# First attention of a four-layer stack: row sums from the exponentials' accumulator, rows scaled by GpSimd ahead of their transposes

## What is computed

```python
x = x + tanh(g_xattn[0]) * _L0_xattn_ref(_layernorm(x), ctx_1024, ctx_1024, mask, wq, wk, wv, wo, bo)

def _L0_xattn_ref(q, k, v, mask, wq, wk, wv, wo, bo):
    HEAD = 16                      # 16 heads of 16 columns
    qh = (q @ wq).reshape(N, Lq, HEAD, HEAD_DIM)
    kh = (k @ wk).reshape(N, Lk, HEAD, HEAD_DIM)
    vh = (v @ wv).reshape(N, Lk, HEAD, HEAD_DIM)
    scores = jnp.einsum('nqha,nkha->nhqk', qh, kh)
    scores = jnp.where(mask == 0, -10000000000.0, scores)
    attn = softmax(scores / math.sqrt(HEAD_DIM), axis=-1)
    out = jnp.einsum('nhqk,nkha->nqha', attn, vh).reshape(N, Lq, D_MODEL)
    return out @ wo + bo
```

## Time and profile before

| | |
|---|---|
| Median of three runs | 1626.49 us |
| Span of the profiled execution | 1600.8 us |
| TensorE busy with matmuls, whole span | 1386.6 us (87%) |
| VectorE, ScalarE, GpSimd busy, whole span | 60%, 42%, 26% |
| Layer 0's attention | the first 195 us or so |

### The profile page before, as it was taken

One profiled execution on the slowest core, in us unless ns is written; L12 is line 12 of the kernel. 1 busy time (PEld: TensorE's weight loads), 2 busy tenths in 40 slices (PEclk: granted clock), 3 DMA queues, 4 the chain that ended last, 5 costly groups with the idle time before them and its releaser, 6 DMA issues. The chain is left out here.

```text
span 1600.8 us, 31601 instructions
## 1 busy us (share of the span) xinstructions
PE 1386.6 (87%) x10662; PEld 1150.0 (72%) x10662; DVE 953.2 (60%) x2331; ACT 664.8 (42%) x1313; POOL 422.6 (26%) x578
## 2 busy tenths in 40 slices
PE   8999878889999994999999998999999997401588
PEld 5888645677799983788888887779999996400245
DVE  4888665666422225777777774832222265688887
ACT  3666453420344430333333334335555522430277
POOL 1000000012122210122221221246666633421141
PEclk9999999899799997999999998889999999755799
DMA  3000020673111107111111202012333344421001
GB/s 107 21 20 15 6 92 1 218 268 61 60 34 41 34 22 226 62 51 49 49 47 32 44 1 93 1 52 92 92 93 93 86 173 134 108 19 10 1 14 40
DMA packets 105328, 106.53 MB, mean 67 GB/s; under 512 B 36080, under 2 KB 92160, under 8 KB 105088
## 3 DMA queue, kind: packets, MB, share of 16 engines
q1 hardware_dynamic: 89312, 70.91, 14.6%
q0 software_dynamic: 11136, 28.93, 6.6%
q10 hardware_dynamic: 4768, 5.25, 1.1%
HBM read 83.19 MB, written 20.71 MB: 65 GB/s over the span
## 5 line engine op out<-in xcount | busy, mean ns | idle before, releaser
L3598 PEld LDWEIGHTS L2f_bank<-L2f_xT,L2f_w_tile 128*128 128x128 f32 x1264 | 154.5, 193 | 7.4 <-ACT L2f_xT L3662 3.4
L3598 PE MATMUL L2f_bank<-L2f_xT,L2f_w_tile 128*128 128x128 f32 x1264 | 155.2, 276 | 3.0 <-ACT L2f_xT L3662 3.0
L785 POOL TENSOR_TENSOR L2x_probs<-L2x_probs,L2x_inv_sum 128x512 f32<-128x512 f32 x64 | 66.3, 1057 | 268.4 <-DVE L2x_inv_sum L1062 268.4
L3712 DVE TENSOR_TENSOR L2f_hT<-L2f_gate_h,L2f_bank 128x256 f32<-128x256 f32 x79 | 33.3, 421 | 148.5 <-ACT L2f_gate_h L3669 148.5
L3521 POOL DMA_INDIRECT L2f_y_rows<-L2f_xn,L2f_put_row x79 | 78.2, 989 | 55.2 <-DVE L2f_xn L3728 51.6
L3656 ACT COPY L2f_w_tile<-L2f_w_up 128x1024 f32 x79 | 82.7, 1046 | 17.4 <-issue 17.4
L3513 POOL DMA_INDIRECT L2f_rows<-L2f_x_rows,L2f_take_row x79 | 77.0, 975 | 44.7 <-DVE L2f_take_row L3496 21.3
L3598 PEld LDWEIGHTS L1f_bank<-L1f_xT,L1f_w_tile 128*128 128x128 f32 x736 | 85.6, 192 | 1.1
L3598 PE MATMUL L1f_bank<-L1f_xT,L1f_w_tile 128*128 128x128 f32 x736 | 85.9, 275 | 0.0
L3615 PE MATMUL L1f_bank<-L1f_w_down,L1f_hT 128*128 x368 | 83.1, 379 | 0.0
L3615 PE MATMUL L2f_bank<-L2f_w_down,L2f_hT 128*128 x316 | 81.4, 380 | 0.1
(11 more groups left out here) (677 smaller groups left out, 3321.2 us busy)
## 6 DMA issues: line engine op xcount, KB each, us to landing
L1f_w_up<-in_L_ffn_w SPq DMA_DIRECT2D x16, 512.0 KB, 8.2
L1f_w_down<-in_L_ffn_w SPq DMA_DIRECT2D x16, 512.0 KB, 9.0
L2f_got<-L2f_y_rows SPq DMA_DIRECT2D x16, 512.0 KB, 4.4
L2f_w_up<-in_L_ffn_gate_w SPq DMA_DIRECT2D x16, 256.0 KB, 2.9
L2f_w_up<-in_L_ffn_up_w SPq DMA_DIRECT2D x16, 256.0 KB, 3.0
L2f_w_down<-in_L_ffn_down_w SPq DMA_DIRECT2D x16, 256.0 KB, 3.6
x<-in_x SPq DMA_DIRECT2D x4, 512.0 KB, 7.9
L0x_ctx<-in_ctx SPq DMA_DIRECT2D x16, 128.0 KB, 2.1
```

What stands on the lines that cost most here:

```text
L785: nc.gpsimd.tensor_tensor(probs[c][:, :, :], probs[c][:, :, :], inv_sum[:, c, :][:, :, None].to_broadcast([P, 4, P]), ALU.mult).then_inc(s ...
L3598: x = nc.tensor.matmul(products(j, m), w_tile[j][:, at:at + P], xT[j][:, k * P:(k + 1) * P], start=(k == 0), stop=(k == KT - 1))
L3712: nc.vector.tensor_tensor(hT[j][:, 0:F], gate_h[j][:, 0:F], bank[2 + j][:, F:2 * F], ALU.mult).then_inc(q["h"], 1)
```

## The change

- `exp` is four instructions, one a head, each with an accumulator output that gives the sum of its row (`row_sum`). The exponentials have four buffers instead of two, and wait for GpSimd's reading of the batch before.
- VectorE takes the reciprocals of these sums (`invert`, 128x4), at four places of its list.
- GpSimd multiplies each group by them (`weigh_rows`) into `weights`, and the transposes read these.
- The product with ones, its operand, its memsets, and the 128x256 reciprocal are gone; `take_heads` is a plain copy.
- The lists are reordered: transposes 2 and 3 of a batch stand behind the scores of the next, front(b+2, T) stands ahead of transposed(b, 1), and ScalarE's copies move likewise.

```diff
--- before.py
+++ after.py
@@ -300,7 +300,8 @@
-        ones32 = sb(f"{tag}_ones32", [P, 2, 32])
+        row_sum = sb(f"{tag}_row_sum", [P, 4, 4])
+        inv_sum = sb(f"{tag}_inv_sum", [P, 4, 4])
@@ -311,16 +312,16 @@
-        probs = [sb(f"{tag}_probs{j}", [P, 4, P]) for j in range(2)]
+        probs = [sb(f"{tag}_probs{j}", [P, 4, P]) for j in range(4)]
+        weights = [sb(f"{tag}_weights{j}", [P, 4, P]) for j in range(2)]
-        inv_sum = sb(f"{tag}_inv_sum", [P, D])
-            "inv", "headsT", "projected", "updated", "passed", "gated_bias", "x_biased"])
+            "inv", "weights", "headsT", "projected", "updated", "passed", "gated_bias", "x_biased"])
@@ -359,26 +360,35 @@
             nc.gpsimd.memset(mask_diag[:, :], 0.0).then_inc(s["diag"], 1)
             for j in range(2):
                 nc.gpsimd.memset(v32[j][:, :, :, :], 0.0).then_inc(s["cleared"], 1)
-            nc.gpsimd.memset(ones32[:, :, :], 0.0).then_inc(s["cleared"], 1)
 
             pool.wait_ge(s["diag"], 1)
             nc.gpsimd.affine_select(out=mask_diag[:, :], in_=mask_diag[:, :], compare_op=ALU.not_equal,
                                     fill=L0_MASK["diag"], base=0, pattern=[[-1, P]],
                                     channel_multiplier=1).then_inc(s["diag"], 1)
 
-            pool.wait_ge(s["cleared"], 3)
-            for odd in range(2):
-                nc.gpsimd.memset(ones32[:, odd, odd * HD:(odd + 1) * HD], 1.0).then_inc(s["cleared"], 1)
-
             def add_bias(j, b, first, last):
 
                 pool.wait_ge(s["xn"], b + 1)
                 nc.gpsimd.tensor_tensor(cols(core.x, b * D, D), cols(core.x, b * D, D), gated_bias[:, :], ALU.add
                                         ).then_inc(s["x_biased"], 1)
 
+            def weigh_rows(b, i):
+
+                pool.wait_ge(s["inv"], b * 4 + (i + 1))
+                after(pool, s["pT"], b * 4 + (i - 1))
+                nc.gpsimd.tensor_tensor(weights[i % 2][:, :, :], probs[i][:, :, :],
+                                        inv_sum[:, i, :][:, :, None].to_broadcast([P, 4, P]), ALU.mult
+                                        ).then_inc(s["weights"], 1)
+
+            def body(j, b, first, last):
+                weigh_rows(b, 0)
+                weigh_rows(b, 1)
+                add_bias(j, b, first, last)
+                weigh_rows(b, 2)
+                weigh_rows(b, 3)
 
             pool.wait_ge(s["gated_bias"], 1)
-            over_batches(pool, add_bias)
+            over_batches(pool, body)
 
         @block.tensor
         def _(pe):
@@ -429,10 +439,10 @@
 
             def transposed(b, i):
 
-                pe.wait_ge(s["exped"], b * 4 + (i + 1))
+                pe.wait_ge(s["weights"], b * 4 + (i + 1))
                 after(pe, s["pT_out"], b * 4 + (i - 1))
                 for h in range(4):
-                    last = nc.tensor.transpose(pT_bank[i % 2][:, h * P:(h + 1) * P], probs[i % 2][:, h, :],
+                    last = nc.tensor.transpose(pT_bank[i % 2][:, h * P:(h + 1) * P], weights[i % 2][:, h, :],
                                                core.ident[:, :])
                 last.then_inc(s["pT"], 1)
 
@@ -441,14 +451,12 @@
                 pe.wait_ge(s["pT_out"], b * 4 + 4)
                 pe.wait_ge(s["evicted"], b * NF + (V + 1))
                 after(pe, s["updated"], b)
-                for at, stationary in ((0, lambda t, i, odd: v32[j][:, 4 * t + i, odd, :]),
-                                       (D, lambda t, i, odd: ones32[:, odd, :])):
-                    for t in range(KT):
-                        for odd in range(2):
-                            for i in range(4):
-                                last = nc.tensor.matmul(out_bank[32 * i:32 * i + 32, at + t * P:at + (t + 1) * P],
-                                                        stationary(t, i, odd), probsT[j][:, i, 2 * t + odd, :],
-                                                        start=(odd == 0), stop=(odd == 1))
+                for t in range(KT):
+                    for odd in range(2):
+                        for i in range(4):
+                            last = nc.tensor.matmul(out_bank[32 * i:32 * i + 32, t * P:(t + 1) * P],
+                                                    v32[j][:, 4 * t + i, odd, :], probsT[j][:, i, 2 * t + odd, :],
+                                                    start=(odd == 0), stop=(odd == 1))
                 last.then_inc(s["pv"], 1)
 
             def project(j, b):
@@ -462,6 +470,7 @@
             def body(j, b, first, last):
                 scores(j, b)
                 if not first:
+                    transposed(b - 1, 2)
                     transposed(b - 1, 3)
                 if has_two_before(b):
                     project(j, b - 2)
@@ -474,16 +483,15 @@
                 transposed(b, 0)
                 if not last:
                     front(1 - j, b + 1, V)
-                transposed(b, 1)
-                transposed(b, 2)
                 if not two_left(b):
                     front(j, b + 2, T)
+                transposed(b, 1)
 
 
             pe.wait_ge(prologue.sems["cleared"], 2)
             stay_warm(core, out_bank, 10)
             pe.wait_ge(s["diag"], 2)
-            pe.wait_ge(s["cleared"], 5)
+            pe.wait_ge(s["cleared"], 2)
             front(0, 0, T)
 
             pe.wait_ge(s["w_q"], 16)
@@ -496,6 +504,7 @@
 
             pe.wait_ge(s["w_o"], 32)
             over_batches(pe, body)
+            transposed(B - 1, 2)
             transposed(B - 1, 3)
             project(0, B - 2)
             weighted(1, B - 1)
@@ -530,9 +539,11 @@
             def exp(b, i):
 
                 act.wait_ge(s["shifted"], b * 4 + (i + 1))
-                after(act, s["pT"], b * 4 + (i - 1))
-                nc.scalar.activation(probs[i % 2][:, :, :], shifted[i % 2][:, :, :], ACT.Exp, scale=scale
-                                     ).then_inc(s["exped"], 1)
+                after(act, s["weights"], (b - 1) * 4 + (i + 1))
+                for h in range(4):
+                    e = nc.scalar.activation(probs[i][:, h, :], shifted[i % 2][:, h, :], ACT.Exp, scale=scale,
+                                             accum_out=row_sum[:, i, h:h + 1])
+                e.then_inc(s["exped"], 1)
 
             def take_pT(j, b, i):
 
@@ -543,6 +554,7 @@
 
             def body(j, b, first, last):
                 if not first:
+                    take_pT(1 - j, b - 1, 2)
                     take_pT(1 - j, b - 1, 3)
                 exp(b, 0)
                 if not last:
@@ -552,11 +564,10 @@
                 exp(b, 2)
                 if not last:
                     take(1 - j, b + 1, V)
-                take_pT(j, b, 1)
                 exp(b, 3)
-                take_pT(j, b, 2)
                 if not two_left(b):
                     take(j, b + 2, T)
+                take_pT(j, b, 1)
 
             prologue.on_scalar(act)
             finish_norm_scalar(core, act, s, temps)
@@ -569,6 +580,7 @@
             take(0, 0, V)
             take(1, 1, T)
             over_batches(act, body)
+            take_pT(1, B - 1, 2)
             take_pT(1, B - 1, 3)
             nc.scalar.preload_act_table(ACT.Sqrt)
 
@@ -598,15 +610,17 @@
                                         top[:, i % 2, :][:, :, None].to_broadcast([P, 4, P]), ALU.subtract
                                         ).then_inc(s["shifted"], 1)
 
+            def invert(b, i):
+
+                dve.wait_ge(s["exped"], b * 4 + (i + 1))
+                after(dve, s["weights"], (b - 1) * 4 + (i + 1))
+                nc.vector.reciprocal(inv_sum[:, i, :], row_sum[:, i, :]).then_inc(s["inv"], 1)
+
             def take_heads(j, b):
 
                 dve.wait_ge(s["pv"], b + 1)
-                nc.vector.reciprocal(inv_sum[:, :], out_bank[:, D:2 * D]).then_inc(s["inv"], 1)
-
-                dve.wait_ge(s["inv"], b + 1)
                 after(dve, s["projected"], b - 1)
-                nc.vector.tensor_tensor(headsT[j][:, :], out_bank[:, 0:D], inv_sum[:, :], ALU.mult
-                                        ).then_inc(s["headsT"], 1)
+                nc.vector.tensor_copy(headsT[j][:, :], out_bank[:, 0:D]).then_inc(s["headsT"], 1)
 
             def update(b):
 
@@ -621,11 +635,16 @@
             def body(j, b, first, last):
                 if not two_left(b):
                     norm(j, b + 2)
+                if not first:
+                    invert(b - 1, 2)
+                    invert(b - 1, 3)
                 shift(b, 0)
                 if has_two_before(b):
                     update(b - 2)
                 shift(b, 1)
+                invert(b, 0)
                 shift(b, 2)
+                invert(b, 1)
                 shift(b, 3)
                 if not first:
                     take_heads(1 - j, b - 1)
@@ -648,6 +667,8 @@
             nc.vector.tensor_scalar(gated_bias[:, :], bo[:, :], core.gate(layer, 0), None, ALU.mult
                                     ).then_inc(s["gated_bias"], 1)
```

(2 more changed lines are left out.)

## The result

The changed kernel is slower. Its median over 4 runs is 1656.05 us (1651.04 to 1656.68), against 1626.96 (1623.12 to 1628.2) of the kernel before beside it: a ratio of 1.0157 [1.0126, 1.0188], +29 us. A second comparison on another occasion gave 1656.52 against 1629.62, 1.0188 [1.0152, 1.0224]. The forecast was 1663 us. What came is near the time of rival 1 (1654): the walked beat of 11.85 us came as 11.82, and the loss of clock that was added to it (+9) didn't take place in the steady part.

A forecast was written before the change was run, and what follows sets the result against it. TensorE was taken to bound layer 0's attention. The profiled span 1600.8 + 27.5 (beats +25.5, stage's end about +2) + 9 for the clock = 1637.3, plus 25.7 from span to median = 1663 us; range 1645 to 1683.

The forecast's parts named there:

- rival 1: Layer 0's attention: slower as walked, without any loss of clock, 1654 us; chance 0.20.
- the walked beat: Layer 0's attention, one batch followed through the engines' queues: 11.85 us against 10.14, +1.7 a batch, +25.5 over 15 beats.
- The bound: Layer 0's attention before the change: TensorE is the bound, with a beat of 10.14 us a batch.
- An exp group: ScalarE: four 128x128 exponentials with accumulator reads take 1.23 us against 0.53, +0.70 a group, +2.8 a batch.
- GpSimd's multiplication: GpSimd, between exp and transpose: four broadcast multiplications of 128x512 at 1.06 us each, 4.2 a batch.
- The memsets: Start of the kernel: five small memsets leave while TensorE warms up, worth nothing.
- The clock term: Layer 0's attention, steady part: TensorE's thin stretch loses clock, 0.6 us a beat, +9 us.
- Rival 2: Layer 0's attention: the clock falls in nearly every beat, some +1.5 a beat, +50, 1676 us; chance 0.17.
- The stage's end: End of layer 0's attention: longer groups +2.8, a VectorE and GpSimd round +1.4, less 2.6: about +2 us.
- Rival 3: Layer 0's attention: TensorE stays the bound as ScalarE takes V early enough; beat 9.25, -13, 1613 us; chance 0.09.
- Rival 4: ScalarE alone sets the beat: its work sums to 8.6 us, under TensorE's 9.25; falls together with rival 3.
- Rival 5: Accumulator reads merged or reciprocals stalled: beat 11.2 to 12.3, 1645 to 1661 us; lower end or mixed cases 0.04.

The follow-up runs named there:

- the change without GpSimd: Changed kernel without GpSimd's multiplication, the transposes reading the exponentials and the rows left undivided: 1663.48 us, ratio 1.018 to the kernel before.
- the old order: Changed kernel's operations with TensorE's and ScalarE's queues in the order of the kernel before: 1681.07 us, ratio 1.0315 to the kernel before.
- the reordered kernel: Changed kernel's same operations, with transposes 1 also behind the next scores and the fills and takes moved earlier: 1622.68 us, again 1625.97.
- one exponential: Changed kernel with one 128x512 exponential a group instead of four, no accumulator, sums a constant 1: 1650.01 us, ratio 1.0097 to the kernel before.
- multiplication twice: Changed kernel with each GpSimd multiplication made twice, the first into a tile nobody reads: 1694.26 us, ratio 1.0379 to the kernel before.

## Why the prediction was right, and where it was wrong

**The bound.** That TensorE bounds the kernel before is shown by the kernel without the product with ones: 0.89 us of work removed, 0.85 of beat gained.

**The walk.** Its stations, counted from the scores' start at 105.83, can be read off the timelines above: take of q and k 4.89 (walked 4.84), exp 1 5.87 (5.82), copy of transposes 0 7.62 (7.6), exp 2 8.10 (8.1), take of V 9.28 (9.3), front T 9.93 (9.85), next scores 11.85 (11.7). The mean of 11.85 was the 11.7 and half of a branch of 0.3 in every second batch. The branch hardly shows: the beats alternate between 11.80 and 11.85, not between 11.7 and 12.0. So the agreement of the mean, to 0.03 us, is in part luck; the walk itself is good to 0.15. Walking the queues anew for the other kernels gave 11.1 where 11.18 was measured, 13.6 for 13.68, 10.8 for 10.78, 10.8 for 10.49, 9.5 for 9.29 and 9.4 to 9.6 for 9.65. It missed most where the clock fell (11.4 to 11.5 for 12.10, 12.9 for 13.55).

**The sizes.** An exp group was put together from two rows as 1.23 (four times 0.30 is 1.20) and measured 1.18. The Trainium skill's figures ("ScalarE: Activation LUTs", section "What ACT_TABLE_LOAD costs") had given an estimate of 0.80 without the accumulator read; the trace disagrees, since a plain slot of 0.21 and 0.09 for the read make the 0.30 of every head. GpSimd's multiplication was put at 1.06 and measured 1.04, 1.5 times the 0.69 of VectorE's subtraction of that size. The "about 2x" of the Trainium skill ("GPSIMD Engine Reference", section 4.1) isn't borne out by this operation, in which one operand is broadcast, and its beat of 12.15 didn't come. With two full operands of 128x512 GpSimd took 1.28 us in the profile of before (layer 2, median of 16), 1.9 times the 0.69, so there the figure fits. The memsets that go are three, not five; they touch nothing either way.

**The clock term, +9: wrong.** This is the step that failed. It put +9 us on the steady part, because that holds a stretch "as thin as the stretch that lost the clock". The stretch is indeed as thin. Busy time in two consecutive stretches of after:

```profile
112.00:114.00 2.00, 1.25 (x8) 1.07 (x8) 1.72 (x5) 1.54 (x10) 1.43 (x2) 1.00 0.00 0
114.00:116.00 2.00, 0.52 (x4) 0.27 (x3) 1.52 (x5) 2.00 (x15) 1.40 (x3) 1.00 0.00 0
```

TensorE was busy 1.25 and then 0.52 us, less than the 1.26 and 0.69 of the earlier trace rows, and the clock stayed at 1.00. One execution in which a thin stretch preceded a fall was taken for a cause that would work in many beats; in the second profile of the same kernel the same stretch precedes no fall. What does make the clock fall stays open. Rival 1 named the case and its time, 1654, and was given 0.20 where it deserved more. Rival 2, a fall in nearly every beat, didn't come in this kernel; falls in the steady part appeared in the change without GpSimd and in the old order.

**The stage's end, +2.** It depends on which profile of before is taken. From the last scores to the next stage's statistics it is 195.88 - 174.33 = 21.55 us in the profile of the prediction, whose clock falls there (mean 0.84), and 18.92 in the second one, at a clock of 1.00. In the changed kernel it is 220.10 - 198.53 = 21.57, and 21.52 in its second profile, both with a fall to 0.50. The last loads and the two ends in the timelines of after:

```profile
198.53 0.98 PEld L435 LDWEIGHTS L0x_bank<-L0x_kT,L0x_qT 32*128 32x128 f32 x32 [0.42 <-issue]
...
220.10 0.19 DVE L237 TENSOR_TENSOR L0f_temps<-stats 128x16 f32<-128x16 f32 x1 [1.01 <-PEq L171]
```

So the end costs 0.0 us by the first pair of profiles and 2.6 by the second. The working took one product with ones and one reciprocal off (2.8 + 1.4 - 2.6 = 1.6, taken as 2), but the end of before holds those of two batches (loads with ones at 178.39 and 188.29), which would make it 2.8 + 1.4 - 5.3 = -1. What the change would cost here at one and the same clock wasn't measured.

**Sum.** From the first scores to the last, the 15 beats together grew by 24.1 us (172.46 against 148.37), where 25.5 was walked: twelve of them by 1.69 each, the first two by 2.3 and 1.1, the last by 0.4. With the end the stage grew by 24.2 and 25.7 in the two pairs of profiles, and 1626.96 with that is 1651 to 1653. The measured 1656.05 is 3 to 5 us above, and its interval holds 1651 to 1653. So the forecast of 1663 is 7 us too high because of the clock term; that it isn't further off is owed to those 3 to 5 us, which it didn't foresee and which may be scatter.

**The rivals.** Rival 3 (the take of V early enough, TensorE bound) needed some 1.75 us off the chain and was rightly held unlikely in this order; by order alone one kernel came near that state (9.65), and another part of the way (10.49). Rival 4, ScalarE's sum of 8.6, is confirmed as no bound by the reordered kernel, where taking 2.8 us off ScalarE changes nothing. Rival 5's lower end (11.2) is near what one exponential gave, 11.18.

## What to carry to other kernels

Work taken off the bounding engine is worth its time only if no chain through the others becomes longer than what is left; so walk one batch through every queue in order, with slots from the trace, before judging by sums of busy time. Where the walk names an instruction that stands behind others it doesn't need (here the take of V behind two groups of exponentials), reorder before giving the change up: the same operations made 1656 us in one order and 1623 to 1626 in another, 0.3% under the kernel before. And one profiled execution is one execution: compare a stage with its own stage, in two profiles of the same kernel first.

## What the runs showed of the hardware that was not expected

- **The clock and pauses.** With the clock at 1.00 throughout the steady part, TensorE stood still for 1.33 and 1.86 us a beat (the change) and 2.45 and 1.86 (multiplication twice, busy 69%). With pauses of 2.42 us and a busy share of 83% it fell to 0.94 on average (no GpSimd), with pauses of up to 1.92 and a share of 78% to 0.90 (old order). Neither the length of a pause nor the busy share of the stage orders these four; what does is open. And it can differ between two executions of one kernel: the stage's end of before at 0.84 in 21.55 us, and at 1.00 in 18.92. A fall took the loads of the scores from 0.98 to 1.80 us, and the beats with it to 12.8 instead of 11.2 (no GpSimd).
- **The accumulator read** lasts 0.196 us by its record and holds the next ACTIVATE up by 0.09: durations of ScalarE's instructions overlap, so distances between starts give the price. Four of them with their 128x128 exponentials take 1.18 us where one of 128x512 takes 0.53.
- **A short VectorE instruction beside GpSimd.** The conversion of the mask (128x128, int32 to bf16) takes 0.22 us in all 16 batches of the kernel before, where GpSimd does little. In the reordered kernel it starts 0.15 us behind a multiplication of GpSimd, takes 0.98 (median of 16) and ends 0.09 behind it:

```profile
110.36 1.04 POOL L379 TENSOR_TENSOR L0x_weights<-L0x_probs,L0x_inv_sum 128x512 f32<-128x512 f32 x1 [1.35 <-DVE L0x_inv_sum L618]
110.51 0.98 DVE L599 TENSOR_SCALAR L0x_mask_add<-L0x_mask 128x128 bf16<-128x128 int32 x1
```

  A 128x512 subtraction out of PSUM beside such a multiplication (105.72 beside 105.18) keeps its 0.69. What is special to the conversion wasn't tested.
- **The same stage, 373 or 401 us.** Layer 2's experts took 7 to 9% longer in every later profile than in the first, with the same instruction counts. Which of its transfers or waits differs wasn't pursued.
